# A two-layer transformer kernel on one core: the memory chunks worked on in pairs over two shared PSUM banks, and a new order of work on every engine

## What is computed

```python
# layer 0
q, k, v = split(h @ Wqkv + bqkv)                      # 16 heads of 8
scores = (q @ k.T + q @ rel_emb.T shifted) / sqrt(8)
x = x + ga * (softmax(scores) @ v @ Wout + bout)
logits = h @ router_w + router_b                      # 16 experts, top 4, softmax of those
x = x + gb * sum_e score_e * ((up_e + 1) * gate_e * sigmoid(1.702 * gate_e)) @ down_e
# layer 1: "memory" attention, 16 heads of 64 = 1024 columns
k = exp(1j * (h @ Wk) * 10);  v = h @ Wv
out_pos   = real(cumsum(v * rotors)        * conj(rotors)) / sqrt(t)
out_assoc = real(cumsum(v * conj(k_shift)) * k)            / sqrt(t)
x = x + ga * ((out_pos * g_pos + out_assoc * g_assoc) @ Wo)
# layer 1: feed-forward
xr, xk = mix(h, h_shifted)
x = x + gb * (sigmoid(xr @ W_r) * (relu(xk @ W_k)**2 @ W_v))
```

## Time and profile before

| | |
|---|---|
| median of 3 runs | 1931.99 us (1931.31 to 1933.45) |
| the profiled execution's own time | 1931.05 us |
| its span in the trace | 1929.3 us |
| TensorE (PE) busy | 1552.5 us, 80% |
| VectorE (DVE) busy | 1280.2 us, 66% |
| ScalarE (ACT) busy | 921.9 us, 48% |
| GpSimd (POOL) busy | 313.8 us, 16% |
| mean granted TensorE clock | 0.883 of full |

### The profile page before, as it was taken

How to read it: one execution, slowest core, us unless ns; L and a number is a source line. 1 busy time by engine, 2 the same in 40 slices (tenths; PEclk the granted TensorE clock), 3 DMA queues, 4 the chain that set the end, 5 groups by cost and what they waited for, 6 DMA issues and landing times.

```text
span 1929.3 us, 24111 instructions
## 1 busy us (share of the span) xinstructions
PE 1552.5 (80%) x7786; PEld 1167.5 (61%) x7786; DVE 1280.2 (66%) x2340; ACT 921.9 (48%) x1476; POOL 313.8 (16%) x261
## 2 busy tenths in 40 slices
PE   3688888788887888888788887788888888887776
PEld 2466656566565666656566665666656666565565
DVE  7566665866667676665866667676665866667666
ACT  1455554444554445444454545445544454544442
POOL 5030301203021120301203021020201203021020
PEclk9889888897988979888898888989888898888988
DMA  6030301102020030200202020030300203011000
GB/s 157 1 28 1 31 2 14 17 0 30 1 24 6 1 29 1 30 1 9 22 0 30 1 19 11 0 30 1 30 1 7 23 0 30 1 15 13 1 3 3
DMA packets 54664, 29.95 MB, mean 16 GB/s; under 512 B 3741, under 2 KB 53610, under 8 KB 54634
## 3 DMA queue, kind: packets, MB, share of 16 engines
q1 hardware_dynamic: 53968, 29.46, 13.4%
q10 hardware_dynamic: 666, 0.11, 0.0%
HBM read 8.20 MB, written 2.10 MB: 5 GB/s over the span
## 4 chain that ended last, share of the span: by engine, by line
PE 43%; issue 22%; DVE 20%; ACT 10%; POOL 4%; DVEq 0%; ACTq 0%; POOLq 0%; DMA 0%
PE ring L633 6%; PE pb L708 4%; PE pb_k L663 4%; DVE gsc L1444 3%; PE pb_v L672 3%; DVE th L1450 3%; DVE prod L1505 3%; PE pa L570 3%; PE pb_k L687 2%; PE ring L557 2%; PE ring L534 2%; PE pb_v L680 2%; PE ring L620 2%; ACT prob L995 2%; PE pb L489 2%
## 5 line engine op out<-in xcount | busy, mean ns | idle before, releaser
L633 PE MATMUL ring<-ht,wgu 128*128 128x256 f32 x1024 | 271.9, 420 | 0.5
L633 PEld LDWEIGHTS ring<-ht,wgu 128*128 128x128 f32 x1024 | 215.3, 213 | 48.1 <-issue 9.8
L376 POOL TENSOR_TENSOR prob<-gsc,sc_all 128x512 f32<-128x512 f32 x128 | 191.5, 1496 | 248.2 <-DVE gsc L1444 124.5
L708 PE MATMUL pb<-prod,wo 128*128 128x256 f32 x768 | 192.9, 402 | 47.2 <-DVE prod L1489 42.4
L645 PE MATMUL pa<-prob,wdown 128*128 128x256 f32 x512 | 166.3, 465 | 59.2 <-DVE prob L1456 58.5
L708 PEld LDWEIGHTS pb<-prod,wo 128*128 128x128 f32 x768 | 151.9, 202 | 74.7 <-DVE prod L1489 45.1
L1378 DVE TENSOR_REDUCE smax<-ring 128x4 f32<-128x1024 f32 x128 | 154.9, 1222 | 49.1 <-PE ring L534 48.4
L995 ACT ACTIVATE prob<-ring 128x1024 f32<-128x1024 f32 x128 | 129.4, 1024 | 113.2 <-PE ring L557 113.0
L645 PEld LDWEIGHTS pa<-prob,wdown 128*128 128x128 f32 x512 | 113.1, 231 | 101.5 <-DVE prob L1456 83.5
L1444 DVE TENSOR_SCALAR gsc<-ring,gub_t 128x256 f32<-128x256 f32 x256 | 111.6, 477 | 94.9 <-PE ring L633 94.9
L1505 DVE TENSOR_TENSOR_SCAN prod<-keep,prod 128x512 f32<-128x512 f32 x128 | 149.3, 1208 | 0.0
(11 more groups left out here) (265 smaller groups left out, 2873.2 us busy)
## 6 DMA issues: line engine op xcount, KB each, us to landing
q_rows<-qk_part SPq DMA_DIRECT2D x144, 64.0 KB
k_rows<-qk_part SPq DMA_DIRECT2D x144, 64.0 KB
x_in<-in_L_attn_x_dram SPq DMA_DIRECT2D x16, 128.0 KB, 2.5
sc_all<-_L_ffn_gate_up_proj_dram SPq DMA_DIRECT2D x1, 2048.0 KB, 13.0
out_dram<-xo SPq DMA_DIRECT2D x16, 128.0 KB, 3.2
prob<-in_L_wmod_dram SPq DMA_DIRECT2D x2, 384.0 KB, 4.6
wo<-in_L_attn_Wo_dram SPq DMA_DIRECT2D x1, 512.0 KB, 4.6
wk<-in_L_attn_Wk_dram SPq DMA_DIRECT2D x1, 512.0 KB, 5.4
```

The source lines that it names most:

```text
L376: pool.tensor_tensor(gsx[:, n % 2, :], gsc[:, n % NG, :], sca, ALU.mult).then_inc(S["gsc"], 1)
L633: last = mm(ring[:, n % 2, g * 512 + j * L:g * 512 + (j + 1) * L], lhsT=wgu[:, 2 * n + j, g, :], rhs=ht[:, :], start=True, stop=True, skip ...
L708: last = mm(pb[:, 0:L], lhsT=wo[:, n // 2, 2 * c + j, :], rhs=prod[:, c % 2, n, j * L:(j + 1) * L], start=(c == 0 and n == 0 and j == 0), ...
```

## The change

No arithmetic is added or taken away. Three groups of edits:

1. The chunks' banks. The next batch's q and k products move from `pb_k` to a bank of `ring` (`hp`), its v products from `pb_v` to the free half of `pa` (`head_5` is parted into `head_5` and `head_6`), so `pb_k` and `pb_v` belong to the memory and the feed-forward. Chunks go in pairs: the `phase_values` of an odd chunk go to `pb_k`, and `phases` of an odd chunk wait only for the turns of the one before (`frac`), not for its first product. The sums of a pair wait for the values of both. The absolute value of the turns is taken in place, in `frac`, instead of into `turn`.
2. Helpers are parted so that they can be placed singly: `memory_o`, `memory_c` and `memory_d` do one of their two products each, `memory_s` is the sum, `value` is parted from `phase`, `attn_tail_2` from `attn_tail`, `centre3` and `next_b` from `head_b`.
3. The lists of `step` are written in another order on PE, ACT, DVE and POOL. SyncE's list is as before.

```diff
             def head_5(nx):
                 need(pe, "h1", nx, 1)
-                need(pe, "pr1", nx - 1, 0)
-                need(pe, "pr2", nx - 1, 0)
                 for n in range(2):
-                    last = mm(pb_k[:, n * L:(n + 1) * L], lhsT=wqk[:, n, :, :].rearrange("p d h -> p (d h)"), rhs=hta[:, :],
+                    last = mm(hp[:, n * L:(n + 1) * L], lhsT=wqk[:, n, :, :].rearrange("p d h -> p (d h)"), rhs=hta[:, :],
                               start=True, stop=True, skip_group_check=True)
                 last.then_inc(S["qk_ps"], 1)
+
+            def head_6(nx):
+                need(pe, "norm2", nx, 0)
                 for n in range(NT):
-                    last = mm(pb_v[:, n * D:(n + 1) * D], lhsT=hta[:, n * P:(n + 1) * P],
+                    last = mm(pa[:, L + n * D:L + (n + 1) * D], lhsT=hta[:, n * P:(n + 1) * P],
                               rhs=wqkv_v[:, :], start=True, stop=True, skip_group_check=True)
...
                 if c == 0:
                     need(pe, "h3", b, 1)
-                    k = later(b)
-                    need(pe, "q_sb", b, k)
-                    need(pe, "k_sb", b, k)
-                    need(pe, "v_sb", b, NT * k)
                     need(pe, "ksq", b, 0)
                     need(pe, "rsig", b, 0)
-                    need(pe, "xo", b, 0)
+                elif c == 2:
+                    need(pe, "pr1", b, c)
                 else:
-                    need(pe, "pr1", b, c)
+                    need(pe, "frac", b, c)
...
             def phase_values(b, c):
 
-                if c:
+                if c % 2:
+                    need(pe, "frac", b, c + 1)
+                elif c:
                     need(pe, "pr2", b, c)
+                else:
+                    need(pe, "xo", b, 0)
+                bank = (pb_v, pb_k)[c % 2]
...
             def sums_1(b, c):
                 need(pe, "in1", b, c + 1)
-                need(pe, "frac", b, c + 1)
+                if c % 2:
+                    need(pe, "pr1", b, c)
+                else:
+                    need(pe, "val", b, c + 2)
                 running_sums(b, c, 0, pb_k)
...
-                af(val[:, c % 2, :], pb_v[:, :], ACT.Copy).then_inc(S["val"], 1)
+                af(val[:, c % 2, :], (pb_v, pb_k)[c % 2][:, :], ACT.Copy).then_inc(S["val"], 1)
...
-                af(fabs[:, :], frac[:, h, :], ACT.Abs).then_inc(S["fabs"], 1)
+                need(act, "sin", b, c + 1)
+                af(frac[:, h, :], frac[:, h, :], ACT.Abs).then_inc(S["fabs"], 1)
```

More of the change, by code:

```diff
@@ L774, in step @@
                 if on_a:
-                    scores(a, 6)
+                    scores(a, 7)
                 if on_b:
+                    phases(b, 1)
                     time_values(b, 0)
+                    phase_values(b, 1)
                 if on_a:
-                    scores(a, 7)
                     turn_max(a)
                 if on_b:
+                    time_values(b, 1)
                     sums_1(b, 0)
-                    sums_2(b, 0)
-                else:
+                if not on_b:
                     turn_rotors(0)
@@ L851, in step @@
                     head_2(nx)
+                if on_b:
+                    phases(b, 3)
+                    time_values(b, 2)
+                if on_x:
+                    head_3(nx)
                 if on_a:
                     variance(a, "2", pa, sq)
-                if on_x:
-                    head_3(nx)
                 if on_b:
-                    phases(b, 3)
-                    phase_values(b, 3)
+                    memory_wo(b, 1)
                 if on_a:
@@ L1127, in step @@
                     copy_max(a)
+                if on_b:
+                    value(b, 1)
+                    tables(b, 1)
+                if on_a:
                     exps(a, 0)
@@ L1130, in step @@
                     exps(a, 2)
-                if on_b:
-                    phase(b, 1)
-                if on_a:
                     exps(a, 3)
-                if on_b:
-                    tables(b, 1)
-                if on_a:
                     exps(a, 4)
+                    exps(a, 5)
                     copy_values(a, 0)
-                    for n in range(5, ST):
-                        exps(a, n)
+                    exps(a, 6)
+                    exps(a, 7)
                 if on_b:
@@ L1576, in step @@
                 if on_a:
-                    for n in (3, 4, 5):
-                        maxima(a, n)
+                    maxima(a, 3)
+                    maxima(a, 4)
+                    maxima(a, 5)
                 if on_b:
@@ L1643, in step @@
                 if on_b:
-                    centre(b, "4", x3, centb, pb)
-                    epsilon(b, "4", vepsb, pb)
+                    memory_b(b, 3)
+                    memory_d(b, 2, 3)
+                    memory_o(b, 2, 1)
+                    memory_o(b, 2, 2)
+                    memory_c(b, 3, 3)
+                    memory_c(b, 3, 4)
+                    memory_d(b, 2, 4)
+                    memory_d(b, 3, 4)
+                if on_a:
+                    gate(a, 0)
+                if on_b:
+                    memory_s(b, 2)
+                if on_a:
+                    gate(a, 1)
+                if on_b:
+                    memory_d(b, 3, 3)
+                    memory_o(b, 3, 1)
+                if on_a:
+                    gated(a, 0)
+                if on_b:
+                    memory_s(b, 3)
+                if on_a:
+                    expert_last(a, 0)
+                if on_b:
+                    memory_o(b, 3, 2)
+                if on_x:
+                    head_6(nx)
+                if on_a:
+                    gate(a, 2)
+                    gated(a, 1)
+                if on_b:
+                    memory_end(b)
+                if on_a:
+                    expert_last(a, 1)
+                    gated(a, 2)
+                    gate(a, 3)
+                    expert_last(a, 2)
+                if on_b:
+                    centre(b, "4", x3, centb, pb)
+                if on_a:
+                    gated(a, 3)
+                    gate(a, 4)
+                    expert_last(a, 3)
+                if on_b:
+                    epsilon(b, "4", vepsb, pb)
+                if on_a:
+                    gate(a, 5)
+                    gated(a, 4)
+                    gate(a, 6)
+                if on_b:
                     scale(b, "4", centb, pb)
@@ L1648, in step @@
                 if on_a:
[L1649 to L1657 removed]
+                    gated(a, 5)
+                    gated(a, 6)
+                    expert_last(a, 4)
+                    expert_last(a, 5)
+                    gate(a, 7)
+                    expert_last(a, 6)
+                if on_x:
+                    maxima(nx, 0)
+                if on_a:
+                    gated(a, 7)
+                    expert_last(a, 7)
+                if on_b:
                     mix_out(b)
                 if on_a:
[L1660 to L1663 removed]
                     experts_out(a)
[L1665 to L1666 removed]
+                    centre3(a)
+                    next_b(a)
             run(dve, head, step)
[L1671 to L1673 removed]
 def run(eng, head, step):
```

402 lines of the change are left out of this document (223 added, 179 removed).

## The result

The changed kernel takes 1609.26 us (median, 1607.65 to 1611.82), the kernel before 1931.65 beside it: ratio 0.8333, 95% interval 0.8318 to 0.8348. The prediction was 1742 with a range down to 1655, so the gain was 1.7 times the forecast. The profiled execution took 1608.18 us with a span of 1606.4; the mean clock rose from 0.883 to 0.953.

A forecast was written before the change was run, and what follows sets the result against it. Waits between engines bound the kernel, no engine being full. Periods of 21 + 19 + 64 = 104 us, with 131.6 to the first x2, shorter steps 1 and 15 and a last step of 60.6, gave 1742 us; range 1655 to 1850.

The forecast's parts named there:

- Stage 1: From x2 to the first exponential: 21 us against 21.4, products ahead of `turn_max` showing only 0 to 2 us.
- Stage 2: From the first exponential to the start of the sum making x1: 19 us, bounds 17 and 22, against 29.6.
- Stage 3: From the start of the sum making x1 to the next x2: 64 us, bounds 57.4 and 71, against 65.0.
- The last step: Step with only layer 1: paired chunks fill 7 of VectorE's 27.9 idle us, giving 60.6 us against 67.6.
- Tight packing: Rival: the second and third stages at their bounds, 17 and 59 us; period 97, 1637 us; chance 0.15.
- the blocked VectorE: Rival: GpSimd's `expert_pair` holds VectorE for its whole length, about +6 us; period 110, 1832 us; chance 0.13.
- The low clock: Rival: it stays, first stage 23 us, third at clock 0.87, +3 to +5; period 111, 1847 us; chance 0.12.
- given back in stage 3: Rival: chunks deferred into the experts hold up gates, `down_pair` and x2; 75 us there, period 115, 1907 us; chance 0.07.
- The rows of q and k: Rival: they come late if part 3 passes 88 us into the period; at 90, period 118.5, 1960 us; chance 0.06.

The follow-up runs named there:

- warm_small: The changed kernel with three useless matmuls a period (two before the third norm's variances, one before chunk 0's phases) and 20 in the last step: 1572.04 us.
- fill_wait: The changed kernel with the rest of chunks 0 and 1 moved ahead of `memory_a` of chunk 2 in VectorE's list: 1615.4 us, ratio 0.8347.
- tables_between: The changed kernel with ScalarE's tables of chunk 1 put back between the second and third exponential: 1687.22 us, ratio 0.8715.
- unpaired: The changed kernel with chunks 0 and 1 not paired, chunk 1's tables among the exponentials again: 1725.58 us, ratio 0.893.
- before_filled: The kernel before with 25 useless matmuls a period put where TensorE waits: 1866.46 us, ratio 0.9652.
- pair_late: The changed kernel with each `expert_pair` on GpSimd also waiting for the `gated` before it: 1620.21 us, ratio 0.8386.
- the first sizing: The changed kernel with seven useless matmuls a period and 37 more in the last step, 1585.25 us; with those of the last step alone, 1613.25 us.

## Why the prediction was right in its parts and too cautious in its sum

- **Stage 1**, 21 predicted, 20.3 measured. The products ahead of `turn_max` were covered but for a part: some run at 1.2 GHz, in the stretch from 883 to 890 us, and `warm_small` gets 1.6 us back there.
- **Stage 2**, 19 predicted, 17.8 measured, before 29.6. The exponentials took 10.8 us (11 predicted), x1 came 37.9 us behind x2 (40), VectorE waited 5.05 us for `phase` of chunk 2 (5), and `fill_wait` shows that this wait costs nothing. The loads were worth their 1.28 us. By the Trainium skill (ScalarE: Activation LUTs, What ACT_TABLE_LOAD costs) every switch has a drain of about 1.38 us beside the load. The traces don't agree: in `tables_between` the load starts 0.02 us behind the end of an exponential and the sine 0.01 us behind the load, and in the change the next function starts 0.02 us behind it.
- **Stage 3**, 64 predicted, 55.4 measured: this is the step that failed, the sentence "TensorE: before 54.0; deferred ... +6.4; less low clock, -3: 57.4" and the allowance of 6.6 us in which it stands still. The mechanism was right. TensorE is busy 52.2 and not 57.4: with the 6.4 of deferred work, 54.0 + 6.4 - 52.2 = 8.2 us went and not 3. The earlier trace rows allowed a better estimate: a mean clock of 0.87 is 2 x (1 - 0.87) = 26% of the time at the lower level, 14 us of the busy 54.0 if it were spread evenly, half of which goes at the full clock, 7 us. I took less than half of it, and called a floor (57.4) what was none. A finer cut of the kernel before gives the whole: the four stretches of its stage 3 at the lower level.

```profile
1114.50:1117.65 3.15, 3.15 (x13) 2.67 (x11) 1.58 (x3) 1.49 (x3) 1.08 (x2) 0.51 0.00 0
1128.20:1131.50 3.30, 3.17 (x8) 2.55 (x9) 2.57 (x5) 0.00 (x0) 0.00 (x0) 0.50 0.00 0
1138.25:1145.30 7.05, 7.05 (x22) 4.74 (x23) 1.73 (x4) 3.48 (x5) 1.15 (x1) 0.52 0.28 36
1169.10:1172.60 3.50, 3.36 (x9) 2.35 (x8) 1.83 (x3) 0.00 (x0) 0.00 (x0) 0.51 0.00 0
```

  TensorE is busy 16.7 of these 17.0 us. Half of that is 8.4, and 8.2 went. And it stands still 3.2 us, not 6.6, which had no row behind it. That the deferred chunks give it work at any time is the likely reason; no run takes them away alone. 5.2 + 3.4 = 8.6, the whole of the miss in that stage.
- **The last step**, 60.6 predicted, 66.8 measured, before 67.6: wrong the other way. I took 7 us out of VectorE's 27.9 idle ones. The middle of the step, before and after:

```profile
1871.70:1911.70 40.00, 31.21 (x150) 25.26 (x149) 33.25 (x47) 13.21 (x20) 0.00 (x0) 0.99 0.00 1
...
1550.00:1590.00 40.00, 32.04 (x148) 26.02 (x146) 33.25 (x48) 12.73 (x19) 0.00 (x0) 0.96 0.00 1
```

  VectorE has 33.25 us of work in 40 both times. Without layer 0 beside it the chunks are bound by VectorE: only 6.75 of its 27.9 idle us lie there, the others in the two norms, the first phases and the feed-forward. Beside the old order the new one with its pairs wins nothing here. But the new order needs the pairs: in `unpaired` the last step takes 72.4 us.
- **The sum**: the span came out 133.9 us shorter than predicted: thirteen periods (104 - 93.65) x 13 = 134.5, step 1 7.0, against 6.2 in the last step, 0.7 in step 15 and 0.7 before the first x2.
- **Rivals.** Tight packing, 1637 us with stages of 17 and 59, is what happened, and still went too little far; its chance of 0.15 rested on "strict lists have never been without waits in stage 3", which is a habit and not a row. The rule of the Trainium skill behind the blocked VectorE (SBUF — State Buffer, Who interferes with whom) holds in kind: but for one, every `gated` and `expert_last` that started inside a pair was held, and what reads PSUM wasn't. But who starts first keeps its time, and the new list has few such instructions in second place, 18 where the old one had 94: `gated` and `expert_last` took 8 x (1.853 - 1.437) = 3.3 us a period less, where the rival had 6 more. The low clock didn't stay: 2 x (1 - clock) over the stages gives 27 us of a period before, 7 after. Nothing was given back in stage 3. The rows of q and k didn't decide: part 3 was done 62 us into the period, 26 short of the 88 from which they would.

How much of the 21.5 us is order and how much clock, the runs don't part cleanly: each part undone brings back waits and with them low clock. `before_filled` bounds the clock alone from below at 4.2 us a period, with its own 10.8 us of work against it. Step 15, which prepares no next batch, is 3.3 us longer than a period, where before it was 7.8 shorter. Here too the clock is in it. Step 15 of the change and of `pair_late`:

```profile
1443.20:1540.10 96.90, 86.62 (x456) 65.80 (x454) 70.02 (x132) 53.22 (x87) 16.44 (x12) 0.91 0.01 3
...
1454.93:1546.51 91.58, 79.51 (x460) 60.72 (x458) 70.33 (x131) 53.29 (x86) 15.62 (x12) 1.00 0.01 3
```

The same work takes 5.3 us less at the full clock. What kept the clock up in `pair_late` isn't shown.

## What to carry to other kernels

Where TensorE has waits of some microseconds all over a period, its busy time isn't a floor: work out from the clock of each stage how much of the busy time is at the lower level, and take half of that off before calling the rest a bound. The mean clock of a stage gives a first estimate (7 us here), the stretches at the lower level a better one (8.4, and 8.2 came). Look for work of another kind standing between instructions of a chain on one engine (sines between exponentials, a norm before the first gate), and pull it ahead or push it in among work that doesn't hang on it; a wait of the engine that isn't the bound can stay. Where waits are unavoidable, one to four useless matmuls in them can pay, sized by their measured duration and not longer than the wait: the first sizing, about twice the second, cost the last step 2.4 to 3.5 us, the second took 3.0 off it.
